# A four-layer graph network: the order of the steps in a group of edge tiles, on PE, DVE, ACT and SP

## What is computed

```python
xl = (x @ Wl + bl).reshape(n, heads, out_ch)
xr = (x @ Wr + br).reshape(n, heads, out_ch)
e = leaky_relu(xl[src] + xr[dst], 0.2)
score = einsum('ehc,hc->eh', e, att)
smax = segment_max(score, dst)
ex = exp(score - smax[dst])
denom = segment_sum(ex, dst)
alpha = ex / (denom[dst] + 1e-16)
out = segment_sum(xl[src] * alpha[:, :, None], dst)
```

## Time and profile before

| | us |
|---|---|
| median of 3 runs | 7027.55 (7026.99 to 7033.46) |
| profiled execution | 7022.54 |
| its span | 7020.8 |

### The profile page before, as it was taken

How to read it: one execution, slowest core, us unless ns; L and a number is a source line. 1 busy time by engine, 2 the same in 40 slices (tenths; PEclk the granted TensorE clock), 3 DMA queues, 4 the chain that set the end, 5 groups by cost and what they waited for, 6 DMA issues and landing times. The chain is left out here.

```text
span 7020.8 us, 92560 instructions
## 1 busy us (share of the span) xinstructions
PE 4784.8 (68%) x26631; PEld 3982.4 (57%) x26631; DVE 4949.8 (71%) x14309; ACT 1541.5 (22%) x4903; POOL 4746.8 (68%) x4996
## 2 busy tenths in 40 slices
PE   2555555666665777777688888857777776666666
PEld 2444444555554555555466666656666665566555
DVE  4444443888886777877687777757777775888887
ACT  3333332222222111111112112212222221122112
POOL 3777776777775777776477766547666662777775
PEclk8776676777776788888788899967777776777777
DMA  4444445666665444445455545556666664666665
GB/s 136 173 151 164 164 153 162 210 212 212 213 215 164 152 154 154 160 151 148 127 175 181 171 160 176 164 164 213 202 212 208 209 203 128 223 219 227 220 226 161
DMA packets 407530, 1266.65 MB, mean 180 GB/s; under 512 B 128582, under 2 KB 189766, under 8 KB 320630
## 3 DMA queue, kind: packets, MB, share of 16 engines
q1 hardware_dynamic: 200000, 760.73, 30.3%
q0 software_dynamic: 199760, 495.12, 24.6%
q10 hardware_dynamic: 7270, 4.88, 0.2%
HBM read 1083.37 MB, written 176.98 MB: 180 GB/s over the span
## 5 line engine op out<-in xcount | busy, mean ns | idle before, releaser
L770 POOL DMA_INDIRECT gathered_rows<-table_l,arena x3048 | 2901.8, 952 | 1200.9 <-issue 902.4
L1250 PE MATMUL ps<-dst_side,onehot_t 128*128 x8320 | 1466.6, 333 | 269.7 <-issue 143.1
L1250 PEld LDWEIGHTS ps<-dst_side,onehot_t 128*128 128x128 f32 x8320 | 1313.5, 239 | 448.7 <-issue 364.1
L770 POOL DMA_INDIRECT gathered_rows<-table_l,src_rel_edges x1116 | 1061.4, 951 | 662.1 <-issue 327.8
L1159 DVE TENSOR_TENSOR acc<-acc,ps 128x136 f32 (+2 forms) x4160 | 1208.3, 290 | 399.5 <-PE ps L1296 250.0
L1296 PEld LDWEIGHTS ps<-weighted_rows,onehot 128*128 128x128 f32 x8320 | 1199.5, 219 | 170.4 <-issue 154.3
L1296 PE MATMUL ps<-weighted_rows,onehot 128*128 128x136 f32 (+2 forms) x8320 | 1238.3, 306 | 4.1 <-issue 1.7
L1081 DVE TENSOR_REDUCE scores<-products 128x16 f32<-128x512 f32 (+2 forms) x1040 | 711.4, 684 | 27.0
L893 PE MATMUL ps<-gathered_rows,onehot 128*128 128x128 f32 x1664 | 333.3, 363 | 482.7 <-ACT gathered_rows L830 481.8
L770 POOL DMA_INDIRECT arena<-table_l,src_rel_edges x544 | 516.8, 950 | 212.6 <-issue 160.0
L857 DVE TENSOR_TENSOR acc<-acc,ps 128x128 f32 x832 | 238.6, 287 | 537.2 <-PE ps L893 500.6
(11 more groups left out here) (318 smaller groups left out, 5975.7 us busy)
## 6 DMA issues: line engine op xcount, KB each, us to landing
onehot_t<-onehots_turned SPq DMA_DIRECT2D x260, 1024.0 KB
onehot<-onehots SPq DMA_DIRECT2D x260, 1024.0 KB
onehots<-onehot SPq DMA_DIRECT2D x52, 1024.0 KB, 6.7
onehots_turned<-onehot_t SPq DMA_DIRECT2D x52, 1024.0 KB, 4.3
table_l<-arena SPq DMA_DIRECT2D x50, 1024.0 KB
gathered_rows<-table_l,arena POOLq DMA_INDIRECT x3048, 2.5
segment_flags_sb<-segment_flags SPq DMA_DIRECT2D x1300, 8.2 KB
arena<-type_mask_rows SPq DMA_DIRECT2D x75, 256.0 KB, 5.0
```

Source lines behind the costliest of these rows:

```text
L770: pool.indirect_dma_start(out=home(v, t // GC)[:, t % GC, :], out_offset=None, in_=table, in_offset=bass.IndirectOffsetOnAxis(ap=index[:, ...
L1250: ins = nc.tensor.matmul(ps[:, BZ + k, g * P:(g + 1) * P], e.ohT[:, u, t * P:(t + 1) * P], kRows[:, bass.ds(bs[t % 8], D)], start=not gat ...
```

## The change

There are five edits, none of which adds or removes work. On SP the one-hots of group s - 1 are asked for ahead of the flags of group s, the hooks run are those of a slot earlier (8(s - 1) + h in place of 8s + h), four of them ahead of the flags and four behind the loads, and the loop behind the last slot begins a slot earlier. On DVE the places of the later half's blocks are loaded ahead of the adds of unit 0, where before they were loaded behind those of unit 2. On PE own_rows of part 0 goes ahead of dst_rows of part 1, own_rows of part 1 right behind turn_back and ahead of dst_rows of part 2, and own_rows of part 2 right behind the first three sums. On ACT in pass 4 the key, query and relation copies of a hook go ahead of the layer's copies.

```diff
--- before.py
+++ after.py
@@ -982,17 +982,19 @@
 
             def slot(s, u, q):
                 turned_onehots(s, u)
+                onehots(s - 1, 1 - u)
+                for h in range(HOOKS // 2):
+                    after.sp(sp, HOOKS * (s - 1) + h)
                 flags(s, u)
-                onehots(s - 1, 1 - u)
                 after.load(sp, s)
-                for h in range(HOOKS):
-                    after.sp(sp, HOOKS * s + h)
+                for h in range(HOOKS // 2, HOOKS):
+                    after.sp(sp, HOOKS * (s - 1) + h)
             turned_onehots(0, 0)
             flags(0, 0)
             slot(1, 1, 0)
             turns(slot, 2, NG)
             onehots(NG - 1, (NG - 1) % 2)
-            for x in range(HOOKS * NG, after.end):
+            for x in range(HOOKS * (NG - 1), after.end):
                 after.sp(sp, x)
             after.close(sp)
 
@@ -1210,12 +1212,12 @@
                     product(s, w, qw, 1)
                     score(s, 1)
                 if chain:
+                    bl = late_places[r] = blocks_of(r, 8)
                     unit_of_adds(r, 0, br)
                 after.dve(dve, x + 4)
                 if chain:
                     unit_of_adds(r, 1, br)
                     unit_of_adds(r, 2, br)
-                    bl = late_places[r] = blocks_of(r, 8)
                 after.dve(dve, x + 5)
                 if cur:
                     product(s, w, qw, 2)
@@ -1312,33 +1314,32 @@
                 if chain:
                     turn_scores(r)
                 if cur:
+                    own_rows(s, w, qw, 0)
                     dst_rows(s, w, qw, 1, bs)
                 after.pe(pe, x)
-                if cur:
-                    own_rows(s, w, qw, 0)
                 after.pe(pe, x + 1)
                 if chain:
                     spread_drop(r)
                     turn_back(r)
+                if cur:
+                    own_rows(s, w, qw, 1)
                 after.pe(pe, x + 2)
                 if cur:
                     bs = blocks_of(s, 8)
                     dst_rows(s, w, qw, 2, bs)
                 after.pe(pe, x + 3)
-                if cur:
-                    own_rows(s, w, qw, 1)
                 if chain:
                     e.oh_here[v].wait(pe, a_no, 16 * (rq + 1))
                     for n in range(3):
                         sums(r, v, n)
+                if cur:
+                    own_rows(s, w, qw, 2)
                 after.pe(pe, x + 4)
                 if cur:
                     dst_rows(s, w, qw, 3, bs)
                 if chain:
                     sums(r, v, 3)
                 after.pe(pe, x + 5)
-                if cur:
-                    own_rows(s, w, qw, 2)
                 if chain:
                     sums(r, v, 4)
                     sums(r, v, 5)
@@ -2352,13 +2353,13 @@
 
     def act(self, act, x):
 
-        self.layer_act(act, x)
         for k, d in self.due(x):
             if d == 14:
                 self.take_kv(act, k)
                 self.take_query(act, k)
             elif 16 <= d < 20:
                 self.take_relations(act, k, d - 16)
+        self.layer_act(act, x)
 
     def pe(self, pe, x):
 
```

## The result

| | before | changed |
|---|---|---|
| median of four runs each, us | 7028.79 | 6912.39 (6904.15 to 6912.76) |
| ratio | 1 | 0.9831, interval 0.9814 to 0.9848 |
| span of the profiled execution | 7020.8 | 6902.4 |

What follows compares the result with a forecast made beforehand. Gathers pace passes 1 and 5 and nearly pass 2; PE nears its limit in pass 3, a DVE-PE-ACT chain holds pass 4. Savings 52 + 20 + 42 + 4 = 118 off 7027.55 gave about 6910 us, range 6840 to 7005.

Steps and rivals of the forecast that it cites:

- What bounds each pass: Gathers pace passes 1 and 5; pass 2 can give some 60 us, pass 3 some 135, pass 4 some 205.
- -4 for the ends of passes: Ends of passes 2 to 4, where groups run without gathers: 4 us less.
- Own rows, pass 2: PE in pass 2: earlier own_rows save 3.0 us a pair, 2.4 in middle groups; -52 us (-15 to -60).
- the 65: Pass 2: own_rows savings of 51 us over 17 pairs and 14 over 6, before holding some back.
- Own rows, pass 3: Busier PE in pass 3: 0.75 us x 17 pairs and 1.1 x 6; -20 us (-45 to 0).
- SP's order: SP: four waits for turned one-hots in pass 4 go, 3.3 us; later table writes and masks cost 0.
- The places on DVE: DVE in pass 4: product 2's 0.81 us wait for the register load goes; 0.82 x 23 pairs, 19 us.
- The copies on ACT: ACT in pass 4: relation copies ahead save 0.5 us for 19 pairs and 1.85 for 5, 9.5 + 9.
- The slower rival: SP's queue in pass 3: table write lands late behind two one-hots, ACT and PE wait; 7085 us, chance 0.08.
- upper price of 20.1: SP's queue in pass 3: three 1 MB transfers in a row take 12.9 to 20.1 us.
- The clock rival: PE in passes 3 and 4: without gaps TensorE keeps its upper clock level; 6780 us, chance 0.06.

Runs made afterwards that it cites:

- e7: The changed kernel with own_rows(1) one step further ahead on PE, in front of spread_drop: 6862.11 us, ratio 0.9756.
- e1: The kernel before with the three own_rows moved on PE and nothing else: 6974.33 us, ratio 0.9916.
- e5: The changed kernel with own_rows back in their old places in pass 3: 6907.05 us, ratio 0.9817.
- e4: The kernel before with SP's order alone changed: 7023.89 us, ratio 0.9984.
- e2: The kernel before with the register load of the later half's places moved on DVE and nothing else: 7013.67 us, ratio 0.9969.
- e8: The changed kernel with SP's old order: 6933.10 us, ratio 0.9857.
- e3: The kernel before with the relation, key and query copies ahead of the layer's copies on ACT in pass 4, nothing else: 7026.02 us, ratio 0.9988.
- e12: The changed kernel with SP's old order, except that the one-hots of the group before stay ahead of the flags: 6930.87 us, ratio 0.9851.
- e10: The changed kernel with PE's register load of the later half's blocks ahead of spread_drop, and SP's old order: 6887.99 us, ratio 0.9796.

## Why the prediction came out right, and where its steps failed

*What bounds each pass*: right for 1, 2 and 5. The bound of pass 2, 1081 to 1088, was met at 1081.7. The -4 for the ends of passes is not seen as such: the idle time ahead of the next first gather fell by 2.7 us behind pass 4, and not behind pass 3.

*Own rows, pass 2*: the mechanism was right. A pair fell from 43.96 to 40.62 in groups 4 to 21 (3.3; forecast 3.0) and from 41.43 to 39.57 in groups 22 to 33 (1.9; forecast 2.4). The -52 was too small since I held back part of the 65; -65.7 came through, the whole room to the gathers' pace.

*Own rows, pass 3*: the step that failed. I had seen that PE was near its limit, and yet took 0.75 us a pair from DVE's waits. In groups 34 to 49 a pair takes 44.28 before and after; in groups 22 to 33 it rose by 1.15, where 1.1 less was forecast. DVE's wait for products mostly turned into waits for sums, as the waits of a stretch in mid-pass show, before

```profile
DVE products L1074 <- PE ps L1259: 148.9, 91, 5.1
```

and changed:

```profile
DVE acc L1161 <- PE ps L1298: 97.6, 64, 4.8
DVE products L1076 <- PE ps L1261: 41.1, 44, 2.3
```

PE's own idle time did shrink, but its matmuls took longer by as much or more. The window of groups 34 to 49 in the kernel before, beside that of the changed kernel shown with e7:

```profile
4180.99:4535.25 354.26, 302.94 (x1802) 236.64 (x1800) 283.25 (x851) 73.84 (x224) 234.16 (x247) 0.91 0.56 173
```

From before to after, PE's idle time there fell from 6.42 to 5.52 us a pair, and its busy time rose from 37.87 to 38.76 for the same matmuls, at a granted clock of 0.88 instead of 0.91. In groups 22 to 33 the idle time fell by 1.0 and the busy time rose by 2.1. The forecast held PE's time for the same work fixed, and that is what failed.

The loss in the middle groups comes with own_rows (e1 has all of it, e5 none) and lies in the lower clock: over these groups 0.88 was granted before and 0.84 after. Own_rows are not the only thing that can bring such a loss: SP's order alone took these pairs from 47.19 to 47.80 (e4). Why an order keeps PE longer at the lower level is not settled, nor why groups 0 to 21 of e5 gave back what its middle gained.

*The places on DVE*: right, 18.3 for 19 (e2).

*The copies on ACT*: over-sized, 6.6 alone for 18.5. The wait for the copies went as forecast; what stood next was PE's register load in a burst of transfers, which I had not priced. The parts help each other: alone they give 18.3 + 6.6 + 13.9 = 38.8 in pass 4, the places and the copies together 34.2 (e8) and all three 59.1, or 49 to 59 in the four kernels with that code.

*SP's order*: under-sized, -3.3 for -13.9 alone and -24.9 within the change. I priced it by the waits for DMAs alone. The load's gap, up to 2.1 us in pass 4, was in the trace, put down to issue, and the sum has no term for it there.

*The slower rival* did not come: the write now leaves behind both one-hots, as forecast, but the next relation copy comes 14.8 us later and waits for PE alone, not for the write. SP, ACT and PE in pass 3, timeline of the changed kernel (answers to the earlier trace rows):

```profile
3812.20 0.31 SPq L965 DMA_DIRECT2D onehot_t<-onehots_turned  x1
3812.56 0.43 SPq L971 DMA_DIRECT2D onehot<-onehots  x1
3813.68 0.34 SPq L2117 DMA_DIRECT2D table_l<-arena  x1
...
3828.49 0.66 ACT L2108 ACTIVATE arena<-ps 128x256 f32<-128x256 f32 x2 [4.11 <-PE ps L2086]
```

So three requests of 1 MB took less than 16.3 us; my upper price of 20.1 was too high. The rule of the Trainium skill weighed there ("DMA: Bandwidth & Descriptors", section "Queues, rings and completion order") isn't contradicted by it, but its order was not what decided.

*The clock rival* didn't come with this change: in pass 3 the clock fell, in the late groups from 0.91 to 0.88. But e7, where it rose and gave the larger part of the 61 us, shows that its mechanism is there to be had, once the idle stretch is filled and not merely moved.

## What to carry to other kernels

When an engine is near its own limit, a new order of its work moves other engines' waits from one place to another; look for the idle stretch on that engine itself and put ready work there. A register load shown as "issue" is a step of the chain like any other: put it where its engine waits anyway. And price a moved DMA by what runs beside it, not only by who waits for it.

## What the runs showed that I had not expected

In pass 4 a register load on PE took 0.55 us in one place of the changed kernel, when little was moving, and 1.47 in the same place of e8, when 2 MB had just been asked for (up to 2.6 in e3). What the DMA engines moved meanwhile, in slices of 0.5 us: e8 from 5470 to 5490,

```profile
GB/s 295 262 221 197 74 238 57 106 156 0 213 49 123 139 0 221 41 115 148 0 0 0 0 262 508 279 508 197 213 246 295 426 410 426 376 360 369 319 157 229
```

and the changed kernel from 5448 to 5468,

```profile
GB/s 393 442 410 344 385 402 475 459 360 475 377 344 361 230 98 131 131 49 188 25 0 0 0 17 18 22 18 22 18 16 78 191 0 115 328 442 410 426 475 311
```

In e8 the load, from 5482.10 to 5483.57, falls into slices of 508, 279, 508 and 197 GB/s; in the changed kernel, from 5459.47 to 5460.02, into 0 and 17. Over groups 1 to 50 of pass 4 it is the same: in e8 and e12 the load left a gap in 45 groups each. In 16 of these it took 1.08 us or more, always with 327 to 410 GB/s moving, in the other 29 at most 0.73, with 0 to 266. But the rate alone does not decide it: four loads of the changed kernel took 0.56 with 407 to 426. So that the transfers stretch the load is inferred from these and from e8, e10 and e12; it was not measured by itself, and which of the transfers does it is open.
